# A gated product kept in PSUM: its low half moves from GpSimd to VectorE, and late pieces are spread

## What is computed

```python
def _matmul_lora(x, w, a, b):                  # w + rank-16 term
    return x @ w.T + (x @ a.T) @ b.T
h = _layernorm(x) * (1 + cb) + sb
gate, up = _matmul_lora(h, gate_w, ...), _matmul_lora(h, up_w, ...)
hidden = silu(gate) * up
out = x + gb * _matmul_lora(hidden, down_w, down_a, down_b)
```

## Time and profile before

| | us |
|---|---|
| median of 3 runs | 2279.3 (2279.28 to 2288.31) |
| the profiled execution | 2278.67 |
| its span, first to last instruction | 2276.9 |
| TensorE busy | 2028.3 (89%) |
| VectorE busy | 1445.3 (63%) |
| ScalarE busy | 1043.3 (46%) |
| GpSimd busy | 1540.9 (68%) |

### The profile page before, as it was taken

How to read it: one execution, slowest core, us unless ns; L and a number is a source line. 1 busy time by engine, 2 the same in 40 slices (tenths; PEclk the granted TensorE clock), 3 DMA queues, 4 the chain that set the end, 5 groups by cost and what they waited for, 6 DMA issues and landing times.

```text
span 2276.9 us, 32700 instructions
## 1 busy us (share of the span) xinstructions
PE 2028.3 (89%) x11502; PEld 1835.2 (81%) x11502; DVE 1445.3 (63%) x2119; ACT 1043.3 (46%) x2334; POOL 1540.9 (68%) x959
## 2 busy tenths in 40 slices
PE   7587757887778889989999999999999999999999
PEld 4233226777768889889899898899889999999999
DVE  4675776778666688766778765778757774211111
ACT  3776855656553455454555444555444332210000
POOL 1488879998987877977877866877869886110100
PEclk9788877989989999999999999999999999999999
DMA  9799876777867577666667576667577877787786
GB/s 361 283 376 339 318 273 215 276 266 276 285 231 286 192 266 264 245 242 251 208 237 264 203 255 238 208 237 263 205 246 262 275 247 269 249 300 265 257 289 217
DMA packets 120051, 594.13 MB, mean 261 GB/s; under 512 B 10448, under 2 KB 22992, under 8 KB 80208
## 3 DMA queue, kind: packets, MB, share of 16 engines
q1 hardware_dynamic: 119888, 592.04, 73.8%
HBM read 506.97 MB, written 85.03 MB: 260 GB/s over the span
## 4 chain that ended last, share of the span: by engine, by line
PE 54%; DVE 18%; ACT 9%; issue 7%; POOL 6%; DMA 5%; DVEq 0%; ACTq 0%; SPq 0%; POOLq 0%
PE FP L789 46%; DVE ring L1211 7%; DVE ring L1096 3%; PE FP L672 3%; POOL ring L1332 3%; ACT SC L868 2%; DMA raw<-w_gu 2%; DVE FP L1186 2%; PE FP L750 1%; POOL y L1307 1%; DMA wts<-w_scratch 1%; PE FP L814 1%; ACT sqb L986 1%; DVE hb L1171 1%; ACT wts L889 1%
## 5 line engine op out<-in xcount | busy, mean ns | idle before, releaser
L789 PE MATMUL FP<-xhi,wts 128*128 128x368 f32 (+2 forms) x4224 | 1052.0, 325 | 76.4 <-ACT dtb L991 23.0
L789 PEld LDWEIGHTS FP<-xhi,wts 128*128 128x128 f32 x4224 | 754.3, 193 | 86.4 <-issue 71.3
L1332 POOL TENSOR_TENSOR ring<-ring,c_row 128x736 f32<-128x736 f32 (+2 forms) x336 | 575.3, 1712 | 256.3 <-ACT hst L885 256.2
L789 PE MATMUL FP<-xlo,wts 128*128 128x368 f32 (+2 forms) x2112 | 683.4, 324 | 0.0
L868 ACT ACTIVATE SC<-dtb,aneg 128x368 f32<-128x368 f32 (+2 forms) x768 | 409.4, 538 | 577.4 <-DVE ring L1211 576.9
L789 PE MATMUL FP<-hhi,wts 128*128 128x368 f32 (+5 forms) x2376 | 573.9, 322 | 15.6 <-POOL hlo L1348 5.1
L1211 DVE TENSOR_TENSOR_SCAN ring<-SC,hst,ring 128x368 f32<-128x368 f32 (+1 forms) x640 | 580.0, 948 | 4.2 <-ACT SC L868 3.8
L1307 POOL TENSOR_TENSOR y<-y,ring 128x736 f32<-128x736 f32 (+1 forms) x320 | 555.1, 1735 | 13.9
L789 PEld LDWEIGHTS FP<-hhi,wts 128*128 128x128 f32 (+1 forms) x2376 | 409.3, 186 | 23.8 <-issue 8.5
L789 PEld LDWEIGHTS FP<-xlo,wts 128*128 128x128 f32 x2112 | 408.0, 193 | 1.1
L789 PE MATMUL FP<-hlo,wts 128*128 128x368 f32 (+5 forms) x1188 | 380.1, 320 | 0.0
(11 more groups left out here) (109 smaller groups left out, 1915.9 us busy)
## 6 DMA issues: line engine op xcount, KB each, us to landing
wts<-w_scratch SPq DMA_DIRECT2D x243, 1152.0 KB, 5.2
wts<-w_scratch SPq DMA_DIRECT2D x91, 896.0 KB, 4.9
wts<-w_scratch SPq DMA_DIRECT2D x51, 1024.0 KB, 5.6
w_scratch<-wts SPq DMA_DIRECT2D x43, 1152.0 KB, 8.5
raw<-w_gu SPq DMA_DIRECT2D x43, 576.0 KB, 6.7
modw<-mod_w SPq DMA_DIRECT2D x24, 1024.0 KB, 11.2
w_scratch<-wts SPq DMA_DIRECT2D x16, 896.0 KB, 6.2
w_scratch<-wts SPq DMA_DIRECT2D x9, 1024.0 KB, 8.1
```

The source lines that it names most:

```text
L789: last = mm(out, w, x, start=(start and k == 0 and e == 0), stop=(stop and k == n - 1 and e == 2))
L1332: G.tensor_tensor(buf, buf, over_pair(c_of(k)), ALU.mult).then_inc(g_hc, 1)
```

## The change

The product of an up unit is written back into the unit's own PSUM bank instead of `hid`. ScalarE rounds it from there, VectorE subtracts `hhi` from it and writes `hlo`; GpSimd no longer takes part. The semaphore `g_hlo` goes; `v_prod` counts products, and `v_used` of an up unit is now counted by the low half. VectorE does the low half of unit u-1 behind the pieces of unit u. The bank of an up unit is held one unit longer by the planner. In the last part of the pass the pieces of units 63 and 64 stay at their own units, behind the "begin" of these. The order of the matmuls of 62, 63 and 64 among each other is the same.

```diff
+LATE_PIECES = [LAST_LORA + 1, LAST_LORA + 2]
@@ pieces_at
-    for u in (LAST_LORA + 1, LAST_LORA + 2):
-        at[LAST_LORA] += at[u]
-        at[u] = []
@@ bank_plan
-            order += PIECES[c][u] + [("unit", c, u)]
+            order += [("unit", c, u)] + PIECES[c][u] if u in LATE_PIECES else PIECES[c][u] + [("unit", c, u)]
-  ... + (2 if UNITS[item[2]][0] == "gate" or item[2] == LAST_LORA else 1)
+  ... + (2 if UNITS[item[2]][0] in ("gate", "up", "both") or item[2] in (LAST_LORA, LAST_LORA + 1) else 1)
+        def low_made(engine, c, k):
+            engine.wait_ge(v_used, c * NU + [u for u in range(NU) if UNITS[u][0] in ("up", "both")][k - 1] + 1)
@@ tensor
-                            pe.wait_ge(g_hlo, c * NH + k1 - 1)
+                            low_made(pe, c, k1 - 1)
-                        pe.wait_ge(g_hlo, c * NH + k1)
+                        low_made(pe, c, k1)
+                    if u in LATE_PIECES:
+                        unit(c, u, "begin")
                     for p in PIECES[c][u]:
                         piece(p)
...
@@ scalar
-                        act.wait_ge(g_hlo, c * NH + j - 1)
+                        act.wait_ge(v_prod, c * NH + j - 1)
-                    act.wait_ge(v_used, g + 1)
-                    A(hhi[:, j % PART_MAX, 0:T], hid[:, j % 2, 0:T], ACT.Copy).then_inc(a_hh, 1)
+                    act.wait_ge(v_prod, c * NH + j + 1)
+                    A(hhi[rows, j % PART_MAX, 0:T], FP[rows, BANK["unit", c, u], 0:T], ACT.Copy).then_inc(a_hh, 1)
+                    for p in PIECES[c][u]:
+                        piece(p)
                     if u and last == "lora_down":
                         after(c, u - 1)
-                    for p in PIECES[c][u]:
-                        piece(p)
@@ vector
-  V.scalar_tensor_tensor(out=h, in0=h, scalar=0.5, in1=bank, ...).then_inc(v_used, 1)
+  V.scalar_tensor_tensor(out=bank, in0=h, scalar=0.5, in1=bank, ...).then_inc(v_prod, 1)
+            def low(c, u):
+                ...
+                dve.wait_ge(a_hh, c * (NH + 1) + j + 1)
+                V.tensor_tensor(hlo[rows, k, 0:T], FP[rows, BANK["unit", c, u], 0:T], hhi[rows, k, 0:T].bitcast(F32), ALU.subtract).then_inc(v_used, 1)
-                    if g and last != "gate":
+                    if g and last != "gate" and u not in LATE_PIECES:
                         used(*divmod(g - 1, NU))
...
                     for p in PIECES[c][u]:
                         piece(p)
+                    if u in LATE_PIECES:
+                        used(*divmod(g - 1, NU))
+                    if u == LATE_PIECES[0]:
+                        lora_low(c)
+                    if last in ("up", "both"):
+                        low(*divmod(g - 1, NU))
@@ gpsimd
-            def after(c, u):
-                    ...
-                    G.tensor_tensor(hlo[rows, k, 0:T], hid[rows, j % 2, 0:T], hhi[rows, k, 0:T].bitcast(F32), ALU.subtract).then_inc(g_hlo, 1)
-                    if g:
-                        after(*divmod(g - 1, NU))
```

More of the change, by code:

```diff
@@ L308, in free_at @@
         if kind == "unit":
-            g = item[1] * NU + item[2] + (2 if UNITS[item[2]][0] == "gate" or item[2] == LAST_LORA else 1)
+            g = item[1] * NU + item[2] + (2 if UNITS[item[2]][0] in ("gate", "up", "both") or item[2] in (LAST_LORA, LAST_LORA + 1) else 1)
             return place.get(("unit", *divmod(g, NU)), len(order))
@@ L416, in build @@
         g_prep, g_lo, g_hc, g_add, g_ini = sem("prep_lo_ready"), sem("pass_lo_ready"), sem("state_c_ready"), sem("y_added"), sem("y_started")
[L417 removed]
+        g_h2, v_prod = sem("h2_lo_ready"), sem("hidden_product_ready")
         N_CONST = 6 * 16
@@ L838, in _ @@
                 for u in range(NU):
+                    if u in LATE_PIECES:
+                        unit(c, u, "begin")
                     for p in PIECES[c][u]:
                         piece(p)
[L841 to L844, removed]
+                    if u in (LAST_LORA, *LATE_PIECES):
+                        unit(c, u if u == LAST_LORA else u - 1, "begin" if u == LAST_LORA else "end")
+                        if u == LATE_PIECES[-1]:
+                            unit(c, u, "end")
+                    else:
                         unit(c, u)
@@ L1045, in after @@
                 g, T = c * NU + u, CH[c]
-                if kind == "up":
-                    act.wait_ge(v_used, g + 1)
-                    A(hhi[:, j % PART_MAX, 0:T], hid[:, j % 2, 0:T], ACT.Copy).then_inc(a_hh, 1)
-                elif kind == "both":
-                    act.wait_ge(v_used, g + 1)
-                    A(hhi[0:HALF, j % PART_MAX, 0:T], hid[0:HALF, j % 2, 0:T], ACT.Copy).then_inc(a_hh, 1)
+                if kind in ("up", "both"):
+                    rows = slice(0, P if kind == "up" else HALF)
+                    act.wait_ge(v_prod, c * NH + j + 1)
+                    A(hhi[rows, j % PART_MAX, 0:T], FP[rows, BANK["unit", c, u], 0:T], ACT.Copy).then_inc(a_hh, 1)
                 elif kind == "lora_down" and part == len(PARTS) - 1:
@@ L1233, in used @@
                     dve.wait_ge(v_used, g)
-                    V.scalar_tensor_tensor(out=h, in0=h, scalar=0.5, in1=bank, op0=ALU.mult, op1=ALU.mult).then_inc(v_used, 1)
+                    V.scalar_tensor_tensor(out=bank, in0=h, scalar=0.5, in1=bank, op0=ALU.mult, op1=ALU.mult).then_inc(v_prod, 1)
                 elif kind == "both":
@@ L1240, in used @@
                     dve.wait_ge(a_up, c + 1)
-                    V.scalar_tensor_tensor(out=h, in0=h, scalar=0.5, in1=tda[0:HALF, 0:T], op0=ALU.mult, op1=ALU.mult).then_inc(v_used, 1)
+                    V.scalar_tensor_tensor(out=bank[0:HALF, :], in0=h, scalar=0.5, in1=tda[0:HALF, 0:T], op0=ALU.mult, op1=ALU.mult).then_inc(v_prod, 1)
                 elif kind == "lora_down":
@@ L1251, in used @@
                         else:
-                            dve.wait_ge(g_hlo, (c + 1) * NH)
+                            low_made(dve, c, NH)
                             V.tensor_tensor(hid[at, NH % 2, 0:T], of, tda[at, 0:T], ALU.add).then_inc(v_used, 1)
@@ L1258, in used @@
                                            op0=ALU.mult, op1=ALU.add).then_inc(v_used, 1)
+            def low(c, u):
+                kind, part, j = UNITS[u]
+                T, k = CH[c], j % PART_MAX
+                rows = slice(0, P if kind == "up" else HALF)
+                dve.wait_ge(a_hh, c * (NH + 1) + j + 1)
+                V.tensor_tensor(hlo[rows, k, 0:T], FP[rows, BANK["unit", c, u], 0:T], hhi[rows, k, 0:T].bitcast(F32), ALU.subtract).then_inc(v_used, 1)
             def lora_low(c):
@@ L1287, in _ @@
                         used(*divmod(g - 2, NU))
-                    if g and last != "gate":
+                    if g and last != "gate" and u not in LATE_PIECES:
                         used(*divmod(g - 1, NU))
-                    if UNITS[u][:2] == ("down", len(PARTS) - 1) and UNITS[u][2] == 0:
-                        lora_low(c)
                     for p in PIECES[c][u]:
                         piece(p)
+                    if u in LATE_PIECES:
[4 more added lines that the diff above has]
+                        low(*divmod(g - 1, NU))
             used(CHUNKS - 1, NU - 1)
```

## The result

The changed kernel takes 2328.7 us (median; 2324.2 to 2331.8), the one before 2279.3: a ratio of 1.022, 95% interval 1.020 to 1.025. The forecast was 2316 and slower. The profiled execution has a span of 2327.3 us, against 2276.9.

What follows compares the result with a forecast made beforehand. TensorE, busy 89% of the span, was taken as the bound, so only idle time in passes 0 to 3 could move. Pass 0's +11 and +8.8 each in passes 1 to 3 gave +37, 2316 us; range 2253 to 2350.

Steps and rivals of the forecast that it cites:

- The handshake's price: Behind a group of pieces, VectorE's low half waits for ScalarE's rounded copy: 1.26 us each, 16 to 20 times per pass.
- 10.4 - 1.4 = 9.0 us exposed: Second stretch, passes 1 to 3: 10.4 us added VectorE time, less 1.4 us it waits for TensorE, lengthens each pass.
- The planner's line: Up units' banks come free only with the low half, so most units reuse another bank; no cost of its own.
- The other stretches: Passes 1 to 3: first stretch's 12.3 us hidden; third costs 3.5 us, half of 6.9 exposed.
- VectorE's time alone: Low half on VectorE, 22 per pass: 0.59 us each (0.45 in pass 0), summed together with the waits for rounding.
- Pass 4: 39 us of VectorE's new work and waits fit into its 32.3 and 30.8 us of waits for TensorE: zero cost.
- GpSimd's relief: First stretch of pass 0: eight fewer GpSimd instructions of 0.72 us save 5.8 us; nothing in passes 1 to 5.
- The last units: Waits for the squares and late low half go: 7.2 us saved in pass 0, 3.7 each in passes 1 to 3.
- some 3 us before TensorE wants it: Last units: VectorE makes the last low half after three pieces instead of seven, early enough that TensorE's wait goes.
- 18 + 3 x 12.5 = +55: Loss before the last units' gain: 18 us in pass 0, 9.0 + 3.5 us in each of passes 1 to 3.
- The rival of relief: VectorE's 37% idle time takes all its new work, leaving a 24 us gain over the run, 2255 us; chance 0.18.
- no slack anywhere: All three stretches of passes 0 to 3 feel VectorE's added time in full: +89 us, about 2368 us; chance 0.10.

Runs made afterwards that it cites:

- e1: Changed kernel, but ScalarE rounds the product of unit u-1 ahead of its pieces of unit u, not behind them; 2301.3 us.
- e5: e2 with the planner holding the banks of up units one unit longer, no instruction added or removed; 2292.1 us.
- e11: e2 with VectorE making each up unit's product twice, banks held as before; 2290.8 us.
- e8: e1 with VectorE's low half cut to 16 columns, the rest of hlo zeroed once ahead of pass 0; 2296.2 us.
- e6: e2 without the low halves of the hidden tiles, hlo set to zero once ahead of pass 0; 2256.2 us.
- e2: The spread kernel, or spread alone: kernel before with only the pieces of units 63 and 64 moved to their own units, GpSimd making the low half; 2270.9 us.
- e3: Changed kernel with the old grouping, all pieces of units 62 to 64 ahead of unit 62; 2336.4 us.
- e4: e1 with the tanh of a gate unit also moved ahead of ScalarE's pieces; 2257.5 us.
- e7: e2 with the tanh moved ahead of ScalarE's pieces, GpSimd making the low half; 2238.7 us.
- e9: e1 with VectorE's low half ahead of its own pieces, and the planner holding banks as in the kernel before; 2328.8 us.
- e12: e11 with the planner also holding the banks of up units one unit longer; 2308.7 us.

## Why the prediction came out right, and where it did not

The direction and the time (2316 against 2329) held, and of the mechanism one half: VectorE does wait for the rounding as forecast. Where that wait is felt, and what lengthens the second stretch, it had wrong. Point by point:

- **The handshake's price** was 1.26 us at 16 to 20 places per pass; it was 1.1 us at 19 to 22 (133 us, 121 times). Right, a little too few. Not all of it is new idle time: VectorE's wait for the tanh fell from 234 to 196 us.
- **Where it is felt.** Here the prediction was wrong. The step "10.4 - 1.4 = 9.0 us exposed" in the second stretch gave the right number, 8.8 us measured, for the wrong reason: with the wait removed (e1) the stretch stayed at 74.8 us, and with nothing but the longer hold (e5) it was at 72.9. The planner's line, which I had read and named, I had priced at nothing of its own. Its term was +21 us over the run; in the second stretches of passes 0 to 3 alone e5 is 26 us longer than the spread kernel. The handshake was felt elsewhere: e1 gave back 14.0 us in pass 0, 5.4 in pass 1 and 5.1 in pass 4, and 1.9 in passes 2 and 3 together, for which I had counted the same handshakes as in pass 1.
- **The other stretches** came near the forecast. In passes 1 to 3 the first changed by -0.7, +5.5 and +0.1 us (0 forecast), the third by +3.7, +4.7 and +4.4 (3.5 forecast).
- **VectorE's time alone** I had not separated from the handshake. It costs 20 us by e11, made ahead of the pieces; by e8, in its own place, 5 to 8 us for some 0.37 of its 0.54 us, so some 7 to 12 for the whole by proportion.
- **Pass 4** was not free: +5.1 us, all of it the handshake (299.2 us in e1). VectorE's 63 us of waits for TensorE were not where the 39 us fell.
- **GpSimd's relief** was 5.8 us in the sum, in the first stretch of pass 0; the bound from e6 is 15 to 18 us, and its profile has most of it in the last units.
- **The last units.** The wait for the squares went. The step "some 3 us before TensorE wants it" failed: the low half came 7.0, 3.3, 1.5 and 1.5 us late. The gain of 18 us was 8 (e2, e3).
- **The clock** had no term. In the changed kernel the idle time of pass 2's second stretch grew by 4.3 us (3.7 to 8.0) and its length by 8.8.

The terms as measured, each from its own kernel: spread -8, VectorE's own work +7 to +20, longer hold +18 to +21, handshake +27, relief between 0 and -18: +26 to +60 us, where the change measured +50. The ends are wide because two terms have two values. With the middle of the first (+13), the hold at +20 and half the relief they give some +43. The forecast's terms were two: VectorE's new work and waits, with pass 0's relief already taken off, 18 + 3 x 12.5 = +55, and the last units -18. Measured, the first is 27 + (7 to 20) - (0 to 18) = +16 to +47, so it was forecast 8 to 39 us too high; the gain was 10 us too high; and the hold of the bank, +18 to +21, was missing. The time came near because these errors nearly cancel, and that part is luck. What stays open is how VectorE's own work and the relief share what is left: e1, which has everything but the handshake, is at +30 over the spread alone, of which the hold is 21.

The rival of relief lost. The rival "no slack anywhere" was too high in both stretches that it added in full: 12.3 and 6.9 us per pass against the -0.7 to +5.5 and 3.7 to 4.7 of passes 1 to 3.

## What to carry to other kernels

A moved operation brings three prices that are separate: its own time, the in-order wait for whoever feeds it, and how long its buffers are held. Price each by itself, since the last can cost as much as the others with no instruction changed (21 us here, against 27 for the waits): read from the allocator which user each buffer comes from next, not only whether one is free. And if an engine asks another for something right behind work that the other also has queued, moving the answer ahead of that work is worth trying: it gave 27, 44 and 32 us here (e1, e4, e7), while e9, which moved VectorE's request ahead as well, was 27 us slower than e1. Look for the places where the kernel has the same pattern already, for they may be worth more than the change at hand.

## What the hardware showed that I had not expected

A wait of TensorE can cost more than it lasts, but not every one does. Unit 30 of pass 2 waits 2.47 us both in the kernel before and in the spread kernel; the nine microseconds behind it have a granted clock of 0.81 in the spread kernel (above) and of 1.00 in the kernel before:

```profile
1157.00:1166.00 9.00, 8.27 (x49) 8.30 (x50) 6.26 (x8) 5.90 (x14) 7.49 (x5) 1.00 0.56 216
```

A wait of 2.93 us in e11 was followed by the full clock too. The six waits of 3.8 to 6.3 us that I read in that stretch (two in e1, one each in e4, e5, e12 and the changed kernel) were all followed by a lower clock, 0.62 to 0.82. In e5 4.1 us more of idleness than in the spread kernel made 7.2 us of length. What decides for the shorter waits, these runs do not show.

The changed kernel's TensorE was busy for 2047.3 us with the instructions that took 2028.3 before, at a mean granted clock of 0.938 against 0.947. By these two executions 19 of the 50 us are clock. The kernel before had 0.939 to 0.952 in its other executions, the changed one 0.937 or 0.938 in all four, so the direction is clear and the size is not.
